# Attention scores in groups of four and three over seven PSUM banks, the value sums in one

## The reference, cut to what matters

```
q = split_heads(x @ Wq, S);  k = ...;  v = ...          # 4 images x 8 heads, head dim 16
attn = einsum('bhsd,bhtd->bhst', q, k) * scale + pos_bias  # 3137 x 3137 per head
attn = softmax(attn, axis=-1)
out  = einsum('bhst,bhtd->bhsd', attn, v)
```

## Time and profile before

| | |
|---|---|
| median of the runs | 3097.91 us |
| profiled execution | 3101.1 us, its span 3099.0 us, mean granted clock 0.978 |
| attention stage | 247 to 2584 us |
| ScalarE busy | 2696.4 us (87%), of it exp (L706) 2292.4 us |
| TensorE matmul busy | 2879.0 us (93%) |
| GpSimd, VectorE busy | 766.7 us (25%), 636.0 us (21%) |

### The profile page before, as it was taken

How to read it: one execution, slowest core, us unless ns; L and a number is a source line. 1 busy time by engine, 2 the same in 40 slices (tenths; PEclk the granted TensorE clock), 3 DMA queues, 4 the chain that set the end, 5 groups by cost and what they waited for, 6 DMA issues and landing times. The chain is left out here.

```text
span 3099.0 us, 55504 instructions
## 1 busy us (share of the span) xinstructions
PE 2879.0 (93%) x21844; PEld 869.9 (28%) x21844; DVE 636.0 (21%) x798; ACT 2696.4 (87%) x2867; POOL 766.7 (25%) x1420
## 2 busy tenths in 40 slices
PE   6957999999999999999999999999999996699998
PEld 3531222222222222222222222222222222355555
DVE  4750111111111111111111111111111111655441
ACT  3747999999999999999999999999999994466664
POOL 0221333333323232323333333323232321000000
PEclk9988999999999999999999999999999998799999
DMA  4441111111111111111111111111111101110100
GB/s 105 159 166 37 27 27 27 27 32 35 30 31 29 30 27 27 30 27 27 27 27 27 27 27 34 34 28 30 30 30 27 27 6 29 43 44 24 40 30 21
DMA packets 166069, 117.34 MB, mean 38 GB/s; under 512 B 111318, under 2 KB 156212, under 8 KB 165108
## 3 DMA queue, kind: packets, MB, share of 16 engines
q1 hardware_dynamic: 163780, 107.50, 12.6%
q0 software_dynamic: 2048, 6.43, 0.6%
HBM read 67.42 MB, written 47.75 MB: 37 GB/s over the span
## 5 line engine op out<-in xcount | busy, mean ns | idle before, releaser
L706 ACT ACTIVATE pr<-ps 128x1179 f32<-128x1179 f32 (+1 forms) x2176 | 2292.4, 1139 | 71.7 <-PE ps L650 46.2
L670 PE MATMUL ps<-pr,va 128*32 128x393 f32 x12800 | 1393.8, 507 | 0.0
L626 POOL TENSOR_TENSOR pr<-pr,e_cur 128x310 f32<-128x310 f32 (+19 forms) x1344 | 704.4, 535 | 1656.6 <-ACT pr L706 1622.7
L650 PE MATMUL ps<-qa,ka 48*128 48x393 f16 (+12 forms) x3808 | 700.5, 319 | 93.7 <-DMA qa<-right_rows 38.6
L647 PE MATMUL ps<-qa,ka 51*128 51x393 f16 (+18 forms) x3360 | 628.0, 316 | 22.0 <-ACT pr L706 11.7
L717 DVE COPY o_sb<-ps 128x393 f32<-128x393 f32 x64 | 36.4, 568 | 2089.0 <-PE ps L670 2089.0
L670 PEld LDWEIGHTS ps<-pr,va 128*32 128x32 f32 x12800 | 252.6, 108 | 476.3 <-issue 453.4
L650 PEld LDWEIGHTS ps<-qa,ka 48*128 48x128 f16 x3808 | 189.7, 94 | 675.3 <-ACT pr L706 514.4
L647 PEld LDWEIGHTS ps<-qa,ka 51*128 51x128 f16 (+1 forms) x3360 | 167.0, 94 | 688.0 <-ACT pr L706 684.0
L1401 PE MATMUL ps<-ln_all,w 128*128 128x393 f32 x512 | 180.1, 494 | 4.9 <-ACT hid L1461 4.9
L1461 ACT ACTIVATE hid<-ps,b 128x393 f32<-128x393 f32 x256 | 135.4, 587 | 54.6 <-PE ps L1401 54.1
(11 more groups left out here) (117 smaller groups left out, 938.2 us busy)
## 6 DMA issues: line engine op xcount, KB each, us to landing
qa<-q_halves SPq DMA_DIRECT2D x64, 196.5 KB
ka<-k_halves SPq DMA_DIRECT2D x64, 196.5 KB
att_rows<-o_norm SPq DMA_DIRECT2D x64, 196.5 KB, 2.2
ln_rows<-ln SPq DMA_DIRECT2D x32, 196.5 KB, 3.5
q_halves<-halves SPq DMA_DIRECT2D x32, 196.5 KB, 2.7
k_halves<-halves SPq DMA_DIRECT2D x32, 196.5 KB, 3.6
qa<-q_halves SPq DMA_DIRECT2D x64, 98.2 KB
ka<-k_halves SPq DMA_DIRECT2D x64, 98.2 KB
```

The costliest lines, as they stand in the source:

```text
L626: nc.gpsimd.tensor_tensor(p, p, e_cur[0:keys, par, t:t + z - a], ALU.mult).then_inc(s_band, 1)
L650: last = nc.tensor.matmul(out[:, cut:W], ka[r:r + 48, par, k0:k0 + keys], qa[r:r + 48, par, q0 + cut:q0 + W], start=True, stop=True, tile_ ...
L670: last = nc.tensor.matmul(ps[quad:quad + 32, O_PS + side, 0:W], va[0:keys, par, kt], pr[0:keys, g % SLOTS_PR, j], start=(kt == 0), stop=(k ...
L706: nc.scalar.activation(pr[:, g % SLOTS_PR, 0:m], ps[:, 3 * (g % 2):3 * (g % 2) + m, 0:W], ACT.Exp, scale=1.0 / (LIFT * LIFT)).then_inc(s_e ...
```

## The change

`GMAX` becomes 4. `fast_order` lists all heads in one row of 6400 units, and cuts them into groups of four and three in turn, without regard to sides or heads: 914 groups of four (even numbers; banks 0 to 3), 914 of three (odd numbers; banks 4 to 6) and a last group of two, 1829 in all. A slot of `pr` is four units wide. The value sums of both sides go to bank 7, and one semaphore `s_o` guards it: the first batch of each side waits for the copy of the side before. The half of the array goes by the place in the group (`r = 64 * (j % 2)`). One loop over all groups replaces `pair`; a batch is issued when its last group is four back, the first batch of a side when it is five back. The wait for a head's loads stands at the head's first unit, which may be inside a group. The batches, the band instructions, the copies and the DMAs are the same in number and size.

```diff
-GMAX = 3
+GMAX = 4
...
+    units = [(n, kt, 4 * side + c) for n in range(NBH) for side in range(2) for kt in range(KT) for c in range(4)]
+    groups, u = [], 0
+    while u < len(units):
+        size = GMAX - len(groups) % 2
+        groups.append(list(range(u, min(u + size, len(units)))))
+        u += size
...
-            O_PS = 6
+            O_PS = 7
...
-                    if not (k == 0 and g < AHEAD):
-                        pe.wait_ge(s_exp, k * NG + g - AHEAD + 1)
+                    if g >= AHEAD:
+                        pe.wait_ge(s_exp, g - AHEAD + 1)
                     for j, u in enumerate(groups[g]):
...
+                        if u % HEAD_UNITS == 0:
+                            pe.wait_ge(s_ld[par], (n // 2 + 1) * (NLD * 16))
...
-                        r = 64 * (u % 2)
-                        out = ps[0:keys, 3 * (g % 2) + j]
+                        r = 64 * (j % 2)
+                        out = ps[0:keys, GMAX * (g % 2) + j]
...
-                        pe.wait_ge(s_o[side], at(2 * k + par))
+                        pe.wait_ge(s_o, at(m // KT))
...
+                done = 0
+                for g in range(NG + DELAY + 2):
+                    if g < NG:
+                        scores(g)
+                    while done < NB and group_of[batches[done][-1]] + (done % KT == 0) <= g - DELAY - AHEAD:
+                        values(done)
+                        done += 1
...
+                for g in range(NG):
+                    act.wait_ge(s_score, g + 1)
+                    if g >= SLOTS_PR:
+                        act.wait_ge(s_pv, BATCHES + batches_until(g - SLOTS_PR))
+                    m = len(groups[g])
+                    b0 = GMAX * (g % 2)
+                    nc.scalar.activation(pr[:, g % SLOTS_PR, 0:m], ps[:, b0:b0 + m, 0:W],
+                                         ACT.Exp, scale=1.0 / (LIFT * LIFT)).then_inc(s_exp, 1)
...
-                        nc.vector.tensor_copy(o_sb[:, side], ps[:, O_PS + side, 0:W]).then_inc(s_o[side], 1)
-                        dve.wait_ge(s_o[side], at(2 * k + half // 2 + 1))
+                        nc.vector.tensor_copy(o_sb[:, side], ps[:, O_PS, 0:W]).then_inc(s_o, 1)
+                        dve.wait_ge(s_o, at(n2 + 1))
```

More of the change, by code:

```diff
@@ L1 @@
 from contextlib import ExitStack
+from itertools import accumulate
 import numpy as np
@@ L77, in score_groups, with fast_order @@
     return groups + tail
[L80 to L86, removed]
+def fast_order(NBH, KT):
+    units = [(n, kt, 4 * side + c) for n in range(NBH) for side in range(2) for kt in range(KT) for c in range(4)]
[4 more added lines that the diff above has]
+        u += size
     batches = [list(range(m, m + 4)) for m in range(0, len(units), 4)]
@@ L514, in build @@
             s_pv = primed(ctx, "f_pv", BATCHES)
-            s_o = [primed(ctx, f"f_o{i}") for i in range(2)]
+            s_o = primed(ctx, "f_o")
             s_shuf = semaphore(ctx, "f_shuf")
@@ L524, in build @@
             DELAY = 2
-            units, groups, batches = fast_order(KT)
+            units, groups, batches = fast_order(NBH, KT)
             NG = len(groups)
             NB = len(batches)
-            assert NG == 136 and NB == BATCHES and NG % SLOTS_PR == 0
+            HEAD_UNITS = len(units) // NBH
             group_of = {u: g for g, members in enumerate(groups) for u in members}
@@ L538, in band_parts @@
             def band_parts(u):
-                par, kt, c = units[u]
+                n, kt, c = units[u]
                 lo = kt * P - REACH
@@ L545, in build @@
             banded = [u for u in range(len(units)) if band_parts(u)]
-            NBU = len(banded)
-            def bands_until(m):
-                return sum(1 for u in banded if u <= batches[m][-1])
+            banded_set = set(banded)
+            bands_until = list(accumulate(sum(1 for u in m if u in banded_set) for m in batches))
             def batches_until(g):
@@ L596, in _ @@
                         store_half(2 * k + par, 0)
-                        sp.wait_ge(s_o[1], at(2 * k + par + 1))
+                        sp.wait_ge(s_o, at(4 * k + 2 * par + 2))
                         sp.wait_ge(s_init, 3)
@@ L615, in _ @@
                 pool.wait_ge(s_init, 3)
[L616 to L626, removed]
+                for u in banded:
+                    n, kt, c = units[u]
+                    g, j = place(u)
+                    a, z, t = band_parts(u)
+                    keys = min(P, T - kt * P)
+                    if kt == 0:
+                        pool.wait_ge(s_vld[n % 2], (n // 2 + 1) * 48)
+                    pool.wait_ge(s_exp, g + 1)
+                    p = pr[0:keys, g % SLOTS_PR, j, a:z]
+                    nc.gpsimd.tensor_tensor(p, p, e_cur[0:keys, n % 2, t:t + z - a], ALU.mult).then_inc(s_band, 1)
             @blk.tensor
@@ L630, in _, with scores @@
                 pe.wait_ge(s_init, 3)
[L632 to L636, removed]
-                    if not (k == 0 and g < AHEAD):
-                        pe.wait_ge(s_exp, k * NG + g - AHEAD + 1)
+                def scores(g):
+                    if g >= AHEAD:
+                        pe.wait_ge(s_exp, g - AHEAD + 1)
                     for j, u in enumerate(groups[g]):
-                        par, kt, c = units[u]
+                        n, kt, c = units[u]
+                        par = n % 2
+                        if u % HEAD_UNITS == 0:
+                            pe.wait_ge(s_ld[par], (n // 2 + 1) * (NLD * 16))
                         keys = min(P, T - kt * P)
@@ L652, in scores, with values @@
                     last.then_inc(s_score, 1)
[L654 to L661, removed]
+                def values(m):
+                    n, kt, c = units[batches[m][0]]
+                    par = n % 2
+                    pe.wait_ge(s_exp, group_of[batches[m][-1]] + 1)
+                    if any(u in banded_set for u in batches[m]):
+                        pe.wait_ge(s_band, bands_until[m])
                     if kt == 0:
-                        pe.wait_ge(s_vld[par], (k + 1) * 48)
-                        pe.wait_ge(s_o[side], at(2 * k + par))
+                        pe.wait_ge(s_vld[par], (n // 2 + 1) * 48)
+                        pe.wait_ge(s_o, at(m // KT))
                     for u in batches[m]:
-                        par, kt, c = units[u]
+                        n, kt, c = units[u]
                         keys = min(P, T - kt * P)
@@ L669, in values @@
                         g, j = place(u)
-                        last = nc.tensor.matmul(ps[quad:quad + 32, O_PS + side, 0:W], va[0:keys, par, kt], pr[0:keys, g % SLOTS_PR, j],
+                        last = nc.tensor.matmul(ps[quad:quad + 32, O_PS, 0:W], va[0:keys, par, kt], pr[0:keys, g % SLOTS_PR, j],
                                                 start=(kt == 0), stop=(kt == KT - 1), tile_position=(0, quad))
                     last.then_inc(s_pv, 1)
[L674 to L692, removed]
+                done = 0
[5 more added lines that the diff above has]
+                        done += 1
+                while done < NB:
+                    values(done)
+                    done += 1
             @blk.scalar
@@ L715, in _ @@
                         n2 = 4 * k + half
-                        dve.wait_ge(s_pv, BATCHES + k * NB + KT * (half + 1))
-                        nc.vector.tensor_copy(o_sb[:, side], ps[:, O_PS + side, 0:W]).then_inc(s_o[side], 1)
-                        dve.wait_ge(s_o[side], at(2 * k + half // 2 + 1))
+                        dve.wait_ge(s_pv, BATCHES + k * BATCHES + KT * (half + 1))
+                        nc.vector.tensor_copy(o_sb[:, side], ps[:, O_PS, 0:W]).then_inc(s_o, 1)
+                        dve.wait_ge(s_o, at(n2 + 1))
                         nc.vector.tensor_copy(tick[:, 0:1], o_sb[:, side, 0:1]).then_inc(s_tick, 1)
```

## The result

The changed kernel takes 3004.1 us (median of 4 runs, 3000.6 to 3007.1) against 3097.8 before (4 runs, 3089.5 to 3098.8): ratio 0.970, 95% interval 0.968 to 0.972, 94 us less. Forecast were 2980 in a range of 2958 to 3028, and 118 less. So the side and the range were right, and a fifth of the forecast gain did not come. The range held with help: the forecast's own range, without the rivals, was 2960 to 3003, and 3004 lies just outside it.

What follows compares the result with a forecast made beforehand. Before: a tie of TensorE and ScalarE, 4.16 against 4.13 us per four groups. After: stage 2189 + 13 + 8 + 9 = 2219 us against 2337, 118 less, so 2980 us, range 2958 to 3028.

Steps and rivals of the forecast that it cites:

- the chain: Attention stage before: TensorE steps and ScalarE periods in turn, 8.56 us for 8 groups, 2328 us in all.
- ScalarE's floor: Attention stage after: exps started without waiting, 1.361 us per group of four and 1.033 per three, 2189 us in all.
- Rival C: Exps of four banks overlap less, 1.40 us apart in place of 1.361: 36 us, time 3016; chance 0.05.
- TensorE's block of four at 0.44: Scores on TensorE: a fourth joins the third in the other array half, so the block still takes 0.44 us.
- Rival A: TensorE stays the bound since the fourth score is not free, 0.62 us a block: time 3028; chance 0.09.
- No lateness in the regular part: Steps away from first batches: no scores come late, the nearest by 0.09 us, so this part runs at the floor.
- the 9 that I carried over from the kernel before: Attention stage: 9 us between the 2328 worked out and the 2337 measured before, unexplained and added to the forecast.
- First batches and the one bank: Side boundaries: 54 steps with two batches cost 13 us, lag behind them 8; the single sums bank is covered, costing nothing.
- the 44 us: Wait for the single sums bank at each side if uncovered: 64 x 0.68 = 44 us at most.
- rival B: The one sums bank drains the pipeline at each side: 44 us, time 3024; chance 0.08.
- D: Slower: GpSimd's band instructions become late and hold TensorE and ScalarE, 259 us: time 3240; chance 0.04.
- E: No gain: ScalarE's 129 us loss is not made by TensorE and stays, only 19 us go: 3079; chance 0.03.

Runs made afterwards that it cites:

- experiment 3: The changed kernel with the first batch of each side issued two groups later in place of one: 3097.1 us, 93 more than the changed kernel.
- experiment 5: The changed kernel with the fourth unit of a group in the same half of the array as the third: 3118.4 us, ratio 1.007 to before.
- experiment 2: The changed kernel with batches moved ahead so every side boundary has an empty step, none put off: 2975.9 us, ratio 0.962 to before.
- (1): The changed kernel with a side's first batch issued four groups back like every other, not put off: 2991.2 us, 13 less than the changed kernel.

## Why the prediction was right, and where it was off

*What bounds the kernel: right, with TensorE the heavier side.* Lightening either engine alone helped. ScalarE's work on a side fell by 1.93 us (32 x 0.058 + 2 x 0.038), and the side by 0.86, where the chain gives 0.98: that is 55 us of the stage in place of the 62 expected, and 38 in the runs. TensorE's work fell by 25 x 0.036 = 0.90 us a side, and the side by 0.91, where the chain gives half of it. So TensorE held the pace in more steps than the chain has.

*ScalarE's floor: right.* Ten exps of the kernel after, beginning with a group of four:

```profile
1200.54 12.20 ACT L693 ACTIVATE pr<-ps 128x1572 f32<-128x1572 f32 x10
```

Their forms in the same kernel (busy us, mean ns):

```profile
L693 ACT ACTIVATE pr<-ps 128x1572 f32<-128x1572 f32 x914 | 1458.7, 1596 | 37.5 <-PE ps L649 32.6 <-PE ps L646 0.8
L693 ACT ACTIVATE pr<-ps 128x1179 f32<-128x1179 f32 x914 | 1161.5, 1271 | 8.9 <-PE ps L649 7.0
```

12.20 less the last one's 1.27 is 10.93 for five groups of four and four of three; with 1.033 for a three, a four is 1.360 from the next (forecast 1.361). What I said would show it, a duration of 1.48 to 1.50, is wrong: it is 1.60, and the three grew from 1.16 to 1.27, with starts as far apart as ever. Rival C is out. So is the price by the Trainium skill that stood beside it (ScalarE: Activation LUTs, "What ACT_TABLE_LOAD costs"): the section lets neighbours overlap by about 93 ns, and here a recorded exp ends 0.24 us after the next has started (1.596 - 1.360, 1.271 - 1.033), where it was 0.11 on average in the kernel before.

*TensorE's block of four at 0.44: right* (scores at 1264.97, values at 1265.41 in experiment 3), and experiment 5 shows how much hung on it. Rival A's price of 0.62 for the block was what the unpaired fourth costs (0.61), but it would have been dearer than its 3028: 3118.

*The end of an exp: the term that was mis-sized.* The scores wait for the end of the exp that frees their banks, and the prediction lets it end 0.12 us after the next one starts. In the kernel after it is 0.24 us on average. Three exps around the boundary at 1265 us, one by one:

```profile
1263.24 1.67 ACT L693 ACTIVATE pr<-ps 128x1572 f32<-128x1572 f32 x1
...
1264.60 1.36 ACT L693 ACTIVATE pr<-ps 128x1179 f32<-128x1179 f32 x1
...
1267.41 1.16 ACT L693 ACTIVATE pr<-ps 128x1179 f32<-128x1179 f32 x1
```

The first ends at 1263.24 + 1.67 = 1264.91, 0.31 us after the second has started, and the scores that wait for it start at 1264.97. The third had waited, and lasts 1.16 again. So every margin in the prediction is about 0.12 us too wide.

*No lateness in the regular part: not quite.* The blocks of four had a margin of 0.32 us against a lag of up to 0.23; with 0.24 for 0.12 the margin is 0.20, and the seventh block in a row with a batch is late by 0.03. Measured, the step ahead of it loses 0.037 us on average (164 such steps). In all it cost 12 us away from the boundaries, against the 9 that I carried over from the kernel before. The longer rows of steps with a batch in experiment 2, in which the lag goes on growing, fit this.

*First batches and the one bank: the sum was too small by 17 us.* Forecast were 13 + 8 us, measured are 38 at the boundaries. The step with two batches takes the 1.90 us that were forecast, and its scores are ready 0.55 after they start (0.54 forecast). Two things were missing. In 47 of the 54 such steps the exp that frees the banks ends 0.29 us after the next has started, not 0.12, and the lateness is 0.39 us, not 0.24. And in the other seven the clock is low, for which the sum had nothing: 1.7 to 2.0 us each, 13 in all. Together that is 31 us in the steps with two batches, where I had 13, and 7 behind them, where I had 8. That the bank itself would cost nothing in this order was right: between 600 and 2400 us of the kernel after no value matmul waits for the copy.

The rule on rotating banks in the Trainium skill (Perfetto Trace Analysis, "Optimizing Tensor Performance", Matmuls) would have had the 44 us paid. With an empty step at the boundary it is nothing (experiment 2), with the tightest order 28 us, a part of it spells (1). So rival B is out at its size.

*Rivals D and E:* no wait of TensorE for GpSimd appears between 600 and 2400 us of the kernel after, and E's 3079 is far.

The sum over the steps: floor 2189, boundaries 38, elsewhere 12, start 2: 2241, where 2219 was forecast. The whole kernel missed by about as much, 24 us: the stage began 5.5 us earlier in the profile after, which was not forecast, while that execution was 3.5 us under the median of its kernel, where the one before was 3.2 above.

## What to carry to other kernels

When two engines both look full, compare their cost for one round of the pattern, then walk the round step by step: a tie costs both, and an average over the round hides what a double buffer can't smooth (5). Widening the groups paid here less by the instructions saved (19 us) than by the array half that the fourth matmul fills for nothing. Where a shared buffer needs a moment to be emptied, move an empty step there; delaying the work instead makes a hole and a burst, and spells of low clock came with it. And keep two readings of an instruction apart: the distance of starts says what it costs its engine, the recorded end says when those who wait for it may go on. In a full queue the second grew while the first stood still.

## What the runs showed of the hardware that was not expected

- TensorE's granted clock fell to 1.2 GHz in the attention stage of the kernel before when its matmuls streamed less: with 350 columns of values in place of 393 in spells (0.94 from 600 to 1200 us, matmuls busy 568 of the 600 us), with 200 columns throughout (0.50), and then the kernel took 3604 us against 3093. Less work for TensorE made it 16.5% slower.
- In the changed kernel a spell began after a step without a batch and a hole of 0.68 us, and made the next two batches 2.85 us long in place of 1.53. The same hole at another boundary had no spell behind it; what decides was not found.
- The duration of an exp in the profile is no price. An exp over three banks reads 1.27 us on average in place of 1.16 where it is never kept waiting, at the same distance of 1.033, and one that had waited reads 1.16 in the same kernel. But its end is real: the scores that need its banks start 0.06 us after it.
